# Another order for the attention phase of a gated cross-attention block, with its second layer norm's work placed elsewhere in the feed-forward

## The reference

```python
# _L0_xattn_ref(layernorm(x), ctx, ...)
query = einsum('bnc,dc->bnd', ctx, Wq) + bq      # ctx: 4 x 256 x 128
key = einsum('bnc,dc->bnd', ctx, Wk) + bk
attention = softmax(einsum('bnd,bmd->bnm', query, key), axis=-1)
x = x + tanh(g_xattn) * einsum('bln,bmn->blm', layernorm(x), attention)
# feed-forward, products in float8 e4m3, hidden size 1024
h = layernorm(x)
x = x + tanh(g_ffn) * qdot(gelu(qdot(h, w_gating[0])) * qdot(h, w_gating[1]), w_linear)
```

## Time and profile before

| what | value |
|---|---|
| median of 3 runs | 49.53 us (49.53 to 49.55) |
| the profiled execution | 49.46 us |
| its span, first to last instruction | 47.7 us |
| PE busy | 41.9 us, 88% of the span |
| DVE busy | 34.5 us, 72% |
| ACT busy | 29.4 us, 62% |
| POOL busy | 17.0 us, 36% |
| HBM read, written | 5.90 MB, 1.05 MB |

### The profile page before, as it was taken

How to read it: one execution, slowest core, us unless ns; L and a number is a source line. 1 busy time by engine, 2 the same in 40 slices (tenths; PEclk the granted TensorE clock), 3 DMA queues, 4 the chain that set the end, 5 groups by cost and what they waited for, 6 DMA issues and landing times.

```text
span 47.7 us, 831 instructions
## 1 busy us (share of the span) xinstructions
PE 41.9 (88%) x242; PEld 28.4 (60%) x242; DVE 34.5 (72%) x108; ACT 29.4 (62%) x66; POOL 17.0 (36%) x35
## 2 busy tenths in 40 slices
PE   3999999963999999998999999999999999999000
PEld 1327888824788888772436555756565588863000
DVE  0103639999797979799999990987666999589700
ACT  0642937399897899655699749765555874563000
POOL 3200799039999550600700250000000599002300
PEclk9999999999999999999999999999999999999999
DMA  0499899999999970000000000000000015330092
GB/s 0 61 361 335 308 368 401 340 189 136 89 103 105 105 73 1 0 0 21 0 0 0 0 0 0 0 0 7 0 0 0 0 54 173 112 115 0 0 340 101
DMA packets 3604, 4.64 MB, mean 97 GB/s; under 512 B 400, under 2 KB 2320, under 8 KB 3600
## 3 DMA queue, kind: packets, MB, share of 16 engines
q1 hardware_dynamic: 2448, 3.61, 22.0%
q0 software_dynamic: 864, 0.79, 18.1%
q10 hardware_dynamic: 288, 0.20, 1.3%
HBM read 5.90 MB, written 1.05 MB: 146 GB/s over the span
## 4 chain that ended last, share of the span: by engine, by line
PE 63%; DVE 12%; DMA 10%; SPq 3%; issue 2%; ACT 2%; DVEq 1%
PE bank L640 14%; PE bank L600 14%; PE bank L646 14%; PE bank L665 13%; DMA x_sb<-x 10%; DVE st L415 4%; PE bank L572 4%; DVE nmax L422 2%; PE bank L622 2%; PE bank L565 2%; SPq L209 2%; DVE mv L418 1%; DVE attn L433 1%; ACT xq L349 1%; DVE yo L488 1%
## 5 line engine op out<-in xcount | busy, mean ns | idle before, releaser
L473 DVE SCALAR_TENSOR_TENSOR ap<-bank,gl 128x512 f16<-128x512 f32 (+1 forms) x19 | 11.5, 603 | 3.8 <-PE bank L646 2.2
L358 ACT ACTIVATE gl<-bank 128x512 bf16<-128x512 f32 (+1 forms) x19 | 9.8, 525 | 5.6 <-PE bank L640 5.5
L640 PE MATMUL bank<-xq,wg 128*128 128x512 fp8e4 (+1 forms) x38 | 10.0, 346 | 0.2 <-ACT xq L349 0.2
L646 PE MATMUL bank<-xq,wg 128*128 128x512 fp8e4 (+1 forms) x38 | 10.0, 346 | 0.0
L665 PE MATMUL bank<-wl,aq 128*128 128x256 fp8e4 x64 | 9.7, 273 | 0.1
L665 PEld LDWEIGHTS bank<-wl,aq 128*128 128x128 f16 x64 | 6.1, 98 | 3.5 <-DVE aq L482 0.6
L600 PE MATMUL bank<-attnT,xT_sb 128*128 128x256 f32 x32 | 8.1, 385 | 0.0
L278 POOL TENSOR_TENSOR yo<-ys,x 128x256 f32<-128x256 f32 x4 | 3.0, 776 | 9.3 <-ACT ys L366 9.3
L263 POOL TENSOR_TENSOR r<-ve,neg_half 128x2 f32<-128x2 f32 x4 | 3.0, 759 | 8.5 <-DVE ve L456 8.5
L600 PEld LDWEIGHTS bank<-attnT,xT_sb 128*128 128x128 f32 x32 | 5.6, 190 | 0.7 <-ACT attnT L332 0.2
L482 DVE TENSOR_SCALAR aq<-ap 128x512 uint16<-128x512 uint16 (+1 forms) x19 | 5.7, 302 | 0.0
(11 more groups left out here) (50 smaller groups left out, 54.7 us busy)
## 6 DMA issues: line engine op xcount, KB each, us to landing
x_sb<-x SPq DMA_DIRECT2D x4, 256.0 KB, 4.7
xT_sb<-xT SPq DMA_DIRECT2D x4, 256.0 KB, 5.9
out<-yo SPq DMA_DIRECT2D x6, 128.0 KB, 2.1
wg<-w_gating POOLq DMA_DIRECT2D x4, 128.0 KB, 8.7
par<-params_ctxT SPq DMA_DIRECT2D x1, 256.0 KB, 4.4
wl<-w_linear POOLq DMA_DIRECT2D x2, 128.0 KB, 8.7
out<-yo SPq DMA_DIRECT2D x1, 256.0 KB, 2.0
par<-params_ctxT SPq DMA_DIRECT2D x1, 192.0 KB, 2.7
```

Of the source, the lines that this page charges most:

```text
L358: nc.scalar.activation(gl[:, s % 2, toks], gate_b[s % 2][:, toks], ACT.Gelu_apprx_tanh).then_inc(gelu_ready, 1)
L473: nc.vector.scalar_tensor_tensor(ap[:, s % NAP, toks], up_b[s % 2][:, toks], ACT_SCALE, gl[:, s % 2, toks], ALU.mult, ALU.mult).then_inc(p ...
L640: mm = nc.tensor.matmul(gate_b[s % 2][:, toks], wg8[:, c, k, 0, o:o + P], xq[:, g, k, toks], start=(k == 0), stop=(k == KC - 1))
L646: mm = nc.tensor.matmul(up_b[s % 2][:, toks], wg8[:, c, k, 1, o:o + P], xq[:, g, k, toks], start=(k == 0), stop=(k == KC - 1))
```

## The change

- Attention phase: `k_out` goes from ACT to DVE; all normalising goes to POOL; statistics of x on DVE are taken apart and put behind and between row maxima; energy(1) stands ahead of the second pair of projections; turns wait for each token tile by itself; attend(0) and attend(1) are cut at other places.
- First layer norm: scales in two halves (`scales1(0)`, `scales1(1)`); xs is gone, x2 is made from raw x without the shift nms1. (The second layer norm takes out what is constant over a row.) The shift is added in the end: as the bias of `scale_out`, or in a tile x2s that ACT makes behind steps 7 to 9.
- Second layer norm: batch 0 is normalised by ACT, batch 1 by DVE, 2 and 3 by ACT as before. `X_AFTER` becomes (4, 6); ACT's norm2 stands one step ahead of it. On DVE add_attention(3) goes behind product 0, the moments of batch 2 behind step 1, the statistics of batch 3 behind steps 2 and 3 and its moments behind step 4.
- `scale_out` of batches 0 and 1: four instructions of one tile instead of two. `STEPS` is the same list.

The declarations of tiles and semaphores are left out of the diff.

```diff
     S = len(STEPS)
-    X_AFTER = (3, 6)
+    X_AFTER = (4, 6)
+    ACT_NORM = (0, 2, 3)
...
+        first_of_g1 = next(s for s, step in enumerate(STEPS) if step[0] == 1)
         def last_step(b):
...
-            def shift_x(b):
-                pool.wait_ge(nms1_ready, 1)
-                for t in range(LT):
-                    nc.gpsimd.tensor_scalar(xs[:, b, t], x_sb[:, b, t], 1.0, nms1[:, b, t:t + 1], ALU.mult,
-                                            ALU.add).then_inc(xs_ready, 1)
-            def scales1():
-                pool.wait_ge(mv1_ready, LT * B)
-                nc.gpsimd.tensor_scalar(ve1[:, :, :], mv1[:, :, :, 1], EPS, None, ALU.add).then_inc(ve1_ready, 1)
-                pool.wait_ge(ve1_ready, 1)
-                nc.gpsimd.tensor_tensor(r1[:, :, :], ve1[:, :, :], neg_half[:, :, :], ALU.pow).then_inc(r1_ready, 1)
-                pool.wait_ge(r1_ready, 1)
-                pool.wait_ge(ntg_ready, 1)
+            def scales1(h):
+                pair = slice(h * B // 2, (h + 1) * B // 2)
+                pool.wait_ge(mv1_ready, LT * (h + 1) * B // 2)
+                nc.gpsimd.tensor_scalar(ve1[:, pair], mv1[:, pair, :, 1], EPS, None, ALU.add).then_inc(ve1_ready, 1)
+                pool.wait_ge(ve1_ready, h + 1)
+                nc.gpsimd.tensor_tensor(r1[:, pair], ve1[:, pair], neg_half[:, pair], ALU.pow).then_inc(r1_ready, 1)
+                pool.wait_ge(r1_ready, h + 1)
+                if h == 0:
+                    pool.wait_ge(ntg_ready, 1)
+                nc.gpsimd.tensor_scalar(s1[:, pair], r1[:, pair], tg[:, 0:1], None, ALU.mult).then_inc(s1_ready, 1)
+            def shifts1():
                 nc.gpsimd.tensor_scalar(nr1[:, :, :], r1[:, :, :], ntg[:, 0:1], None, ALU.mult).then_inc(nr1_ready, 1)
-                nc.gpsimd.tensor_scalar(s1[:, :, :], r1[:, :, :], tg[:, 0:1], None, ALU.mult).then_inc(s1_ready, 1)
...
             def rstd2(b):
...
                 nc.gpsimd.tensor_tensor(r2[:, b], ve2[:, b], neg_half[:, 0], ALU.pow).then_inc(r2_ready, 1)
-                if b >= 2:
+                if b in ACT_NORM:
                     pool.wait_ge(r2_ready, b + 1)
-                    pool.wait_ge(nm2_ready, b - 1)
+                    pool.wait_ge(nm2_ready, ACT_NORM.index(b) + 1)
...
             def add_residual(k):
                 b, t = divmod(k, LT)
-                pool.wait_ge(scaled_ready, b + 1)
+                pool.wait_ge(scaled_ready, k + 1)
...
             def load_w_linear(h):
...
             pool.wait_ge(consts_ready, 1)
-            scales1()
-            shift_x(0)
-            shift_x(1)
-            normalise(B - 1)
+            normalise(0)
+            normalise(1)
+            scales1(0)
+            normalise(2)
+            normalise(3)
+            scales1(1)
...
                 rstd2(b)
+                if b == 1:
+                    shifts1()
...
             pool.wait_ge(aq_ready, S)
-            pool.wait_ge(scaled_ready, GB + 1)
+            pool.wait_ge(scaled_ready, LT * GB + 1)
...
         @block.scalar
...
-            def k_out(b):
-                act.wait_ge(k_done, b + 1)
-                nc.scalar.activation(kT[:, b * L:(b + 1) * L], k_b[b % 2][:, 0:L], ACT.Identity,
-                                     bias=bk).then_inc(k_ready, 1)
             def exps(b):
...
-            def shift_x(b):
-                act.wait_ge(nms1_ready, 1)
-                for t in range(LT):
-                    nc.scalar.activation(xs[:, b, t], x_sb[:, b, t], ACT.Identity,
-                                         bias=nms1[:, b, t:t + 1]).then_inc(act_xs_ready, 1)
+            def shift_x2(n):
+                b, t = ((2, 0), (3, 0), (3, 1))[n]
+                if n == 0:
+                    act.wait_ge(nms1_ready, 1)
+                act.wait_ge(x2_ready, LT * b + t + 1)
+                nc.scalar.activation(x2s[:, n], x2[:, b, t], ACT.Identity,
+                                     bias=nms1[:, b, t:t + 1]).then_inc(x2s_ready, 1)
             def norm2(b):
-                act.wait_ge(nmr2_ready, b - 1)
+                act.wait_ge(nmr2_ready, ACT_NORM.index(b) + 1)
...
-            def scale_out(b):
+            def scale_out(b, t):
...
                 act.wait_ge(ffn2_done, last_step(b) + 1)
-                if b == 0:
+                if (b, t) == (0, 0):
                     act.wait_ge(yscale_ready, 1)
-                nc.scalar.activation(ys[:, b].rearrange("p t d -> p (t d)"), y_b[g][i][:, :], ACT.Copy,
+                nc.scalar.activation(ys[:, b, t], halves(y_b[g][i])[:, t], ACT.Identity, bias=nms1[:, b, t:t + 1],
...
             q_out(0)
-            k_out(0)
             q_out(1)
-            k_out(1)
+            exps(0)
             q_out(2)
-            k_out(2)
-            exps(0)
+            exps(1)
             q_out(3)
-            k_out(3)
-            exps(1)
...
             exps(2)
+            attn_out(1)
             exps(3)
-            attn_out(1)
...
             nc.scalar.activation(table[:, :], tg[:, 0:1], ACT.Gelu_apprx_tanh)
-            shift_x(2)
             attn_out(3)
-            shift_x(3)
+            norm2(0)
...
                 gelu(s)
-                if s == X_AFTER[0] - 2:
+                if s == X_AFTER[0] - 1:
                     norm2(2)
-                if s == X_AFTER[1] - 2:
+                if s == X_AFTER[1] - 1:
...
                     xq_out(3)
-                if s == HT + LAG:
-                    scale_out(0)
-                if s == HT + LAG + 1:
-                    scale_out(1)
-            act.wait_ge(ffn2_done, last_step(2) + 1)
-            nc.scalar.activation(ys[:, 2, 1], halves(y_b[1][0])[:, 1], ACT.Copy,
-                                 scale=yscale[:, 0:1]).then_inc(scaled_ready, 1)
+                if X_AFTER[1] < s <= X_AFTER[1] + LT + 1:
+                    shift_x2(s - X_AFTER[1] - 1)
+                if s == first_of_g1 + LAG:
+                    scale_out(0, 0)
+                    scale_out(0, 1)
+                if s == first_of_g1 + LAG + 1:
+                    scale_out(1, 0)
+                    scale_out(1, 1)
+            scale_out(2, 1)
...
         def _(dve):
-            def stats1(b):
-                dve.wait_ge(s_x[b], 16)
-                for t in range(LT):
-                    nc.vector.bn_stats(st1[:, b, t], x_sb[:, b, t]).then_inc(st1_ready, 1)
+            def stats1(b, t):
+                if t == 0:
+                    dve.wait_ge(s_x[b], 16)
+                nc.vector.bn_stats(st1[:, b, t], x_sb[:, b, t]).then_inc(st1_ready, 1)
+            def moments1(b):
...
                     nc.vector.bn_aggr(mv1[:, b, t], st1[:, b, t]).then_inc(mv1_ready, 1)
+            def k_out(b):
+                dve.wait_ge(k_done, b + 1)
+                nc.vector.tensor_scalar(kT[:, b * L:(b + 1) * L], k_b[b % 2][:, 0:L], bk, None,
+                                        ALU.add).then_inc(k_ready, 1)
             def row_max(b):
...
-            def normalise(b):
-                invert_sum(b)
-                dve.wait_ge(rsum_ready, b + 1)
-                for t in range(LT):
-                    nc.vector.tensor_scalar(attn[:, b, t], e[:, b, t], rsum[:, b, t:t + 1], None,
-                                            ALU.mult).then_inc(attn_ready, 1)
-            def add_attention(b):
+            def add_attention(b, tiles=range(LT)):
                 dve.wait_ge(pv_done, b + 1)
-                dve.wait_ge(s1_ready, 1)
-                if b < 2:
-                    dve.wait_ge(xs_ready, LT * (b + 1))
-                else:
-                    dve.wait_ge(act_xs_ready, LT * (b - 1))
-                for t in range(LT):
-                    nc.vector.scalar_tensor_tensor(x2[:, b, t], halves(pv_b[b % 2])[:, t], s1[:, b, t:t + 1], xs[:, b, t],
-                                                   ALU.mult, ALU.add).then_inc(x2_ready, 1)
+                dve.wait_ge(s1_ready, 1 if b < B // 2 else 2)
+                for t in tiles:
+                    nc.vector.scalar_tensor_tensor(x2[:, b, t], halves(pv_b[b % 2])[:, t], s1[:, b, t:t + 1],
+                                                   x_sb[:, b, t], ALU.mult, ALU.add).then_inc(x2_ready, 1)
             def stats2(b, t):
...
                 nc.vector.tensor_scalar(ve2[:, b], mv2[:, b, :, 1], EPS, None, ALU.add).then_inc(ve2_ready, 1)
-                if b >= 2:
+                if b in ACT_NORM:
...
             def norm2(b):
...
-            def finish(b, t):
+            def finish(n):
+                b, t = ((2, 0), (3, 0), (3, 1))[n]
...
                 dve.wait_ge(ffn2_done, last_step(b) + 1)
+                dve.wait_ge(x2s_ready, n + 1)
                 nc.vector.scalar_tensor_tensor(yo[:, b, t], halves(y_b[g][i])[:, t], yscale[:, 0:1],
-                                               x2[:, b, t], ALU.mult, ALU.add).then_inc(y_ready, 1)
+                                               x2s[:, n], ALU.mult, ALU.add).then_inc(y_ready, 1)
...
```

(114 more changed lines are left out.)

## The result

The changed kernel takes 51.48 us (median of 4 runs, 51.22 to 51.67) against 49.53 (49.49 to 49.55) of the kernel before: ratio 1.0391, 95% interval 1.0344 to 1.0438, slower by 1.95 us. Forecast were 50.65 us and a range of 50.0 to 51.4. The direction held; the measured time lies 0.08 us beyond the range's upper end.

A forecast was written before the change was run, and what follows sets the result against it. PE was taken as the bound from the first feed-forward matmul on, and ahead of it a wait chain through the load of x and DVE's statistics. -0.99 + 2.12 = +1.13 on 49.53 gave 50.65 us, range 50.0 to 51.4.

The forecast's parts named there:

- the three places named: Feed-forward on PE: waits of 0.37 before the fourth up, 0.57 before turn_x2(2), 1.25 before turn_x2(3).
- T: Start of ffn1(0), the first feed-forward matmul on PE: forecast at 21.13 us, against 22.12 before.
- The loss: Feed-forward, from the start of ffn1(0) to the matmul behind turn_x2(3): +10.43 against 8.31 before, 2.12 us lost.
- the start of the attention phase: PE's first projections at 0.43 us each, energy(0) staying at 5.76, energy(1) at 6.98, first turn of attention near 10.5.
- the gain of 0.99: Attention phase: ffn1(0) starts 0.99 us earlier, at 21.13; bounds of the gain 0.6 to 1.2.
- scale_out in four instructions: Tail: costs ACT some 0.2 us more beside PE; no effect on the time, +-0.1.
- The 128x4 power: POOL's pow in scales1, attention phase: 1.09 us, on a line between 0.79 (128x2) and 1.68 (128x8).
- rival (b): Attention phase gains only 0.2 us if POOL's 128x4 pow costs 1.68; time 51.4 us; chance 0.18.
- (c): Feed-forward: turn_x2 waits for nothing, the way from moments2 to xh being shorter; faster, 48.9 us; chance 0.07.
- (d): Feed-forward: half the waits, one of them hidden, about the old time; chance 0.05.
- the port rule: DVE's norm2(1) beside POOL's shifts1: lockout would add 0.3 to 0.46 us; forecast took no delay, upper bound 0.46.
- the sum's +1.13: Whole kernel: -0.99 from the attention phase plus 2.12 from the feed-forward, +1.13 us; chance 0.70.

The follow-up runs named there:

- the attention phase alone: The changed kernel with the feed-forward's placement of before (X_AFTER = (3, 6)), keeping its attention phase and late shift: 48.42 us, ratio 0.9773.

## Why the prediction was right or wrong

**The mechanism of the feed-forward held.** PE waits in the three places named, for the reasons given. Times from T, predicted and seen in the profile after (T = 21.80):

| step | predicted | seen |
|---|---|---|
| product(0) | +1.28 | +1.37 |
| product(1) | +2.67 | +2.77 |
| moments2(2) | +3.47 | +3.56 |
| norm2(2) | +5.12 | +5.21 |
| gelu(4) | +6.12 | +6.21 |
| product(4) | +6.75 | +6.87 |
| moments2(3) | +7.55 | +7.68 |
| norm2(3) | +9.20 | +9.33 |
| matmul behind turn_x2(3) | +10.43 | +10.59 |

Every link is there and takes what its row of before said, to 0.03; product(0) begins 0.09 later than I had put it, and that 0.09 runs through to the end of the loop. The loss is 2.28 instead of 2.12. The experiments confirm the links one by one: with DVE's placement taken back there is no wait, with the moments one step earlier the wait of the second round is gone, and with norm2(2) behind gelu(4) the stretch is 0.76 us shorter.

**The term that failed is the start of the attention phase.** The working took PE's first projections "at 0.43 a projection" and left "energy(0) ... at 5.76", and reached T = 21.13. Seen are 0.85 for each of the first ones and energy(0) at 6.77, energy(1) at 7.64 instead of 6.98, and T 0.67 late. The first turn of attention, forecast "near 10.5", is at 11.24. So the gain of 0.99 is 0.32 in the profile after, outside its bounds of 0.6 to 1.2. That pace was read from one profile, in which it had doubled by 4.45 us, and from the earlier trace rows, where "The clock stands at its full level (2.4 GHz) in every slice": the rows of the first passes, 0.43 us apart until then, speak against that reading, and the trace's own record starts at 4.47. Two projections of two passes each, in the profile of before:

```profile
3.44 1.19 PE L549 MATMUL bank<-par 128*128 128x256 f32 x2
4.45 0.61 PE L557 MATMUL bank<-par 128*128 128x256 f32 x2
```

From energy(1) on the replay is good, 14.15 us to T in the forecast and 14.16 seen; where the pace doubled early T was 20.93 and 20.95, 0.2 *earlier* than forecast. The 0.91 by which the attention phase alone is faster in the medians lies near 0.99 partly by luck: in its profile it is 1.17 at T, less 0.23 in the tail. The gain has a condition, and neither the sum nor a rival knew of it. The chain of before ran through the load of x and DVE's statistics, so that energy(0), done at 6.8, was wanted only at 8.5: 1.7 us of slack over PE's start. The change takes that slack away, and with it the cover of an uncertain pace: its chain of waits begins with PE's projections. In the traces this is what moves T, by 0.9 us. That the new kernel's times scatter more for it is not shown: in the first comparison four runs of before lay within 0.06 us and four of after within 0.45, but in the later groups the runs of before spread by 0.46 to 0.71 us too. The working never asked what had hidden PE's first microseconds.

**A small term was missed in the tail.** "Nothing, +-0.1" for scale_out in four instructions is 0.24 here, and 0.17 to 0.26 in the profiles with two and two. ACT runs a pair in 1.01 and 1.04 us where one wide instruction took 0.68; gelu of step 13 and its product come late, and PE waits once for aq, at 41.71. DVE's rounds beside POOL's adds are long as well, but one was before too (0.83 at 37.55). In the profile after:

```profile
38.22 0.28 DVE L474 TENSOR_SCALAR aq<-ap 128x512 uint16<-128x512 uint16 x1
39.52 0.71 DVE L474 TENSOR_SCALAR aq<-ap 128x512 uint16<-128x512 uint16 x1
40.92 0.73 DVE L474 TENSOR_SCALAR aq<-ap 128x512 uint16<-128x512 uint16 x1
```

**Terms and rivals.** k_out on DVE took 0.46 to 0.48, forecast 0.44. The 128x4 power took 1.04, forecast 1.09; rival (b), which rested on 1.68, is out, though its time (51.4) was nearly the measured one, for another reason: that is luck. Rivals (c) and (d) are out: norm2(3) did not begin before T+9.3, and no wait was hidden. For the port rule, POOL's timeline beside norm2(1) on DVE (20.04, pair 0.73):

```profile
19.80 0.32 POOL L256 TENSOR_SCALAR nr<-r,ntg 128x8 f32<-128x8 f32 x1
20.20 0.30 POOL L258 TENSOR_TENSOR nms<-nr,mv 128x8 f32<-128x8 f32 x1
```

The pair is not longer than it was before beside the power. The trace bears out my choice of no delay there. Of the Trainium skill's rule (SBUF — State Buffer, "SBUF: two separate sides") the rounds above look like a case: 0.28 alone, 0.71 beside POOL's 128x256 adds. In the profile of before a round at 38.91, which starts 0.03 ahead of an add, takes 0.28, and that add 0.83 instead of some 0.75. For POOL's short tiles no run here shows a price.

**The range** was missed by 0.08 us. Its upper end, 51.4, was built from POOL's unknown costs, and held nothing for a start that depends on the execution. Against the sum's +1.13 the profiles differ by 2.20: 0.67 more from the start, 0.24 from the tail, 0.16 from the loop. Without any one of the three the median would lie inside; the start is the largest.

## What to carry to other kernels

Statistics that feed a normalisation several engines away have a due time; when a step list is changed or reused, check for each side job the round from its first instruction through every queue to the matmul that wants it, and what waits in those queues behind it. A wait in a strict-order queue can be shortened by putting the waiting instruction later. And when a chain is rerouted off a slow load onto PE's first matmuls, the slack that hid PE's start is gone: read the spacing of those matmuls, and not only the clock's row, and judge such a gain by several profiles of both kernels.

## What the runs showed of the hardware that was not expected

- The float32 passes of 256 columns start 0.43 us apart at first and 0.216 later, in every profile; the 512-column warm-ups run at the slow pace too (0.43 a start). The change falls on the first entry of the trace's record of the granted clock, full level (2.4 GHz), within 0.1 us; so the pace ahead of it, half of that, is the lower level (1.2 GHz), though the page's row prints full there. With warm-up matmuls since 0.77 us the entry came between 4.09 and 6.44 us, in executions of near-identical kernels; without them at 6.47 and 8.49. What decides on it was not settled.
- POOL's power of -0.5 took 0.69 to 0.82 us on 128x2, 1.04 on 128x4 and 1.68 on 128x8.
- In one kernel (51.57 us, add_attention(3) first) DVE left 0.5 us unused between a ready input and the product that wanted it, at 24.45 us, which nothing in the trace explains.
